# A two-layer conditioned convolution and expert layer: the opening in another order

## The reference

```python
# layer 0
c0 = grouped_conv1d(x, weight, taps=9, groups=4) + (cond @ c_weight.T)[:, :, None] + side[None, :, None]
x1 = x + experts(c0; layer 0)
# layer 1: each sample has its own 32x32 mixing matrix
h   = gelu(gelu(cond @ W0 + b0) @ W1 + b1)
att = softmax(h @ W2 + b2)                      # 128 x 8
c1  = einsum('boi,bih->boh', einsum('bk,koi->boi', att, weight), x1) + (att @ bias_k)[:, :, None]
out = x1 + experts(c1; layer 1)

# experts(y): each of the 4096 rows of 512
logits = y @ W_router.T                         # 8 experts, the best 2, softmax over them
out = y @ W_base.T + b_base + 2 * sum over the best 2 of gate_e * (y @ A_e.T) @ B_e.T    # rank 16
```

## Time and profile before

| | us |
|---|---|
| median of three runs | 392.79 |
| the profiled execution's own time | 393.22 |
| its span in the trace | 391.4 |
| TensorE busy | 375.9 (96%) |
| VectorE busy | 206.6 (53%) |
| GpSimd busy | 169.9 (43%) |
| ScalarE busy | 125.6 (32%) |
| mean granted TensorE clock | 0.978 |

### The profile page before, as it was taken

The page is one execution under the profiler, slowest core; times in us unless marked ns, Lnnn a source line. Parts: engine busy times, 40 slices in busy tenths (PEclk is TensorE's granted clock), DMA queues, the critical chain, the costliest instruction groups (busy, mean ns, idle before and its releaser), DMA issues.

```text
span 391.4 us, 8410 instructions
## 1 busy us (share of the span) xinstructions
PE 375.9 (96%) x2648; PEld 365.4 (93%) x2648; DVE 206.6 (53%) x837; ACT 125.6 (32%) x374; POOL 169.9 (43%) x136
## 2 busy tenths in 40 slices
PE   8785999999999999999999999999999999999996
PEld 6465899999999999999999999999999999999896
DVE  2935355545555455555565455555554555555545
ACT  2631323332333233322333233323332333223331
POOL 3172155335533554345434553455335543454450
PEclk9868799999999999999999999999999999999999
DMA  7986223444433433443433443444334334433101
GB/s 258 308 240 172 95 76 127 122 149 123 147 113 114 147 121 122 146 147 121 117 119 139 132 135 121 147 124 144 116 112 147 121 121 147 145 123 107 54 28 54
DMA packets 45019, 51.91 MB, mean 133 GB/s; under 512 B 11280, under 2 KB 27440, under 8 KB 45008
## 3 DMA queue, kind: packets, MB, share of 16 engines
q1 hardware_dynamic: 45008, 51.78, 41.7%
HBM read 34.70 MB, written 17.06 MB: 132 GB/s over the span
## 4 chain that ended last, share of the span: by engine, by line
PE 89%; SPq 3%; DMA 3%; DVE 2%; issue 1%; ACT 0%; DVEq 0%; ACTq 0%
PE ps_out L398 35%; PE ps_out L410 22%; PE ps_out L432 11%; PE ps_conv L353 7%; PE ps_mix L446 7%; PE ps_conv L358 4%; DMA y_scratch<-y 1%; SPq L292 1%; PE ps_out L453 1%; PE ps_t L419 1%; PE ps_out L419 1%; DMA x_raw<-in_x_phase 1%; DMA scratch<-mix_nat 1%; SPq L309 1%; SPq L304 1%
## 5 line engine op out<-in xcount | busy, mean ns | idle before, releaser
L398 PE MATMUL ps_out<-wa,yT 128*128 128x392 f32 x756 | 154.8, 352 | 1.5 <-DVE res L817 0.8
L398 PEld LDWEIGHTS ps_out<-wa,yT 128*128 128x128 f32 x756 | 130.7, 190 | 4.0 <-DVE res L817 1.3
L410 PE MATMUL ps_out<-wb,yT 128*128 128x256 f32 x756 | 102.9, 285 | 0.0
L410 PEld LDWEIGHTS ps_out<-wb,yT 128*128 128x128 f32 x756 | 94.3, 190 | 0.0
L953 POOL TENSOR_TENSOR yT<-y_raw,yT 128x512 fp32r<-128x512 f32 x31 | 39.5, 1274 | 97.5 <-ACT yT L549 97.5
L964 POOL TENSOR_TENSOR base_bias<-passed,bias 128x512 f32<-128x512 f32 x31 | 39.9, 1288 | 95.8 <-ACT passed L600 95.8
L432 PE MATMUL ps_out<-lb_w,hwT 128*128 128x256 f32 x384 | 56.2, 282 | 0.8 <-ACT hwT L549 0.8
L432 PEld LDWEIGHTS ps_out<-lb_w,hwT 128*128 128x128 f32 x384 | 52.1, 189 | 1.4 <-issue 0.8
L959 POOL TENSOR_TENSOR xb<-x_tok,bias 128x512 f32<-128x512 f32 x32 | 41.0, 1283 | 10.0 <-DMA bias<-in_bias 10.0
L549 ACT ACTIVATE hwT<-ps_t 128x128 fp32r<-128x128 f32 x32 | 8.9, 278 | 103.7 <-PE ps_t L419 103.7
L781 DVE MAX8 top<-ps_out 128x8 f32<-128x8 f32 x64 | 10.8, 169 | 58.9 <-issue 57.4
(11 more groups left out here) (101 smaller groups left out, 339.4 us busy)
## 6 DMA issues: line engine op xcount, KB each, us to landing
x_raw<-in_x_phase SPq DMA_DIRECT2D x31, 384.0 KB, 3.2
x_tok<-in_x_tok SPq DMA_DIRECT2D x32, 256.0 KB, 2.6
y_scratch<-y SPq DMA_DIRECT2D x31, 256.0 KB, 2.3
y_raw<-y_scratch SPq DMA_DIRECT2D x31, 256.0 KB, 2.7
out<-res SPq DMA_DIRECT2D x31, 256.0 KB, 2.0
wa_raw<-in_wa SPq DMA_DIRECT2D x2, 784.0 KB, 4.9
wb_raw<-in_wb SPq DMA_DIRECT2D x2, 512.0 KB, 5.7
lb_raw<-in_lb SPq DMA_DIRECT2D x2, 256.0 KB, 4.9
```

The source lines that it names most:

```text
L398: last = mm(out_banks(y, t)[:, 0, 0:AR + DH], features(y, t, dp)[:, k, :], wa[y][:, wp, k, :], start=(n == 0 and k == 0), stop=(n == len(S ...
L410: last = mm(out_banks(y, t)[:, 1, OUT], features(y, t, dp)[:, k, :], wb[y][:, wp, k, :], start=(n == 0 and k == 0), stop=False, skip_group ...
```

## The change

SyncE issues `x_raw` for tile 1 and all loads behind it without waiting for `x_first`, which gets a semaphore of its own. `x_raw` of tiles 2 and 3, `y` of tiles 1 and 2, the layer 1 weights, the four `mix` rows, the broadcasts, `lb1` and `bias1` stand in another order. The biases of all samples are made by a third product of their own, from a copy of the condition in which the samples are sorted by their place in the tile, so that each broadcast reads one whole run of 4 KB. The products for tiles 0 and 1 and their addition come first. TensorE runs conv(1) ahead of `kernel_scores`, has two of its nine dummy products later, and transposes the probabilities ahead of the last quarter of tile 0's first product. Tile 0's low-rank transpose uses another bank and comes ahead of its second product. GpSimd makes four of the sixteen sorting copies (ScalarE five instead of seven, VectorE seven instead of nine). VectorE and ScalarE split the weights in another order.

```diff
+POOL_MOVES = [(2, 2), (2, 3), (3, 2), (3, 3)]
...
 @block.sync
-            sp.dma_start(x_first[:, :, :], d["x_phase"][0]).then_inc(x_loaded, 16)
+            sp.dma_start(x_first[:, :, :], d["x_phase"][0]).then_inc(x_first_loaded, 16)
             sp.dma_start(pack[:, :], d["pack"]).then_inc(l_pack, 16)
-            sp.wait_ge(x_loaded, 16)
             sp.dma_start(x_raw[:, :, :], d["x_phase"][1]).then_inc(x_loaded, 16)
...
             sp.dma_start(bias[0][:, :], d["bias0"]).then_inc(l_bias[0], 16)
-            sp.wait_ge(cb_ready, 1)
+            load_x(2)
+            store_y(1)
+            sp.dma_start(wa_raw[1][:, :, :], d["wa1"]).then_inc(l_wa[1], 16)
+            load_y(1)
+            sp.dma_start(wb_raw[1][:, :, :], d["wb1"]).then_inc(l_wb[1], 16)
+            sp.wait_ge(cb_ready, 2)
             sp.dma_start(d["bias_scratch"], some_bias[:, 2, :]).then_inc(bias_stored, 16)
-            store_y(1)
-            load_weights(1)
-            load_y(1)
-            sp.wait_ge(bias_stored, 16)
-            for n in range(SPT):
-                sp.dma_start(conv_bias[n::SPT, :, :],
-                             d["bias_scratch"][n::SPT, :].unsqueeze(0).to_broadcast([NB, TILES, C])
-                             ).then_inc(l_bias_conv, 16)
-            sp.dma_start(lb_raw[1][:, :], d["lb1"]).then_inc(l_lb[1], 16)
-            sp.dma_start(bias[1][:, :], d["bias1"]).then_inc(l_bias[1], 16)
-            load_x(2)
             load_tok(1)
...
+            sp.wait_ge(bias_stored, 16)
+            for n in range(SPT):
+                sp.dma_start(conv_bias[n::SPT, :, :],
+                             d["bias_scratch"][n * TILES:(n + 1) * TILES, :].unsqueeze(0).to_broadcast([NB, TILES, C])
+                             ).then_inc(l_bias_conv, 16)
+            load_x(3)
+            store_y(2)
             sp.dma_start(d["scratch"], mix_nat[:, :]).then_inc(mix_stored, 16)
+            load_y(2)
+            sp.dma_start(lb_raw[1][:, :], d["lb1"]).then_inc(l_lb[1], 16)
+            sp.dma_start(bias[1][:, :], d["bias1"]).then_inc(l_bias[1], 16)
             sp.wait_ge(mix_stored, 16)
...
-            store_y(2)
-            load_y(2)
-            load_x(3)
+            store_y(3)
             load_tok(2)
-            store_y(3)
             load_y(3)
 @block.tensor
-            keep_busy(9)
+            keep_busy(7)
             conv(0)
...
-            pe.wait_ge(cond_ready, 2)
-            for n, cond in enumerate((some_cond[:, 0, :], some_cond[:, 1, :], condT)):
-                last = mm(ps_mix[:, 0, n * C:(n + 1) * C], cond, cw_sb, start=True, stop=True)
-            last.then_inc(cb_mm, 1)
+            pe.wait_ge(cond_ready, 3)
+            for n in range(2):
+                biases_product(n, some_cond[:, n, :]).then_inc(cb_mm, 1)
...
+                biases_product(2, some_cond[:, 2, :]).then_inc(cb_mm, 1)
...
+            conv(1)
             kernel_scores()
-            conv(1)
-            first_product_0()
-            turn_probabilities()
+            keep_busy(2)
+            first_product_0(before_last=turn_probabilities)
             mixing_setup()
+            pe.wait_ge(cb_ready, 2)
+            turn_hw(0, 0)
             second_product_0()
-            turn_hw(0, 0)
             b_product(0, 0)
 @block.scalar
-            for n in range(SPT - 1):
-                move_first(3, n)
+            move_first(3, 0)
             probabilities()
             high_wa_part(0, FIRST_KS)
             high_wa_part(0, LAST_KS)
             high_wb(0)
+            high_lb(0)
             weigh(0, 0)
-            high_lb(0)
...
+            turned_hw(0, 0)
             high_y(1)
-            turned_hw(0, 0)
 @block.vector
-            for n in range(SPT):
-                move_first(2, n)
-            move_first(3, SPT - 1)
+            move_first(2, 0)
+            move_first(2, 1)
+            move_first(3, 1)
             scores()
             conv_out(1)
             probabilities()
+            turned_probabilities()
+            choose(0, 0)
+            biases(2, 1, 2)
             low_wa_part(0, FIRST_KS, 1)
-            turned_probabilities()
+            gate(0, 0)
             low_wa_part(0, LAST_KS, 2)
-            choose(0, 0)
-            low_wb(0)
-            gate(0, 0)
             mixing_biases()
             low_lb(0)
             turned_hw(0, 0)
-            low_wa_part(1, FIRST_KS, 1)
+            low_wb(0)
             middle(0)
             conv_out(2)
-            low_wa_part(1, LAST_KS, 2)
+            low_wa_part(1, FIRST_KS, 1)
             choose(0, 1)
             turned1(0)
             gate(0, 1)
+            low_wa_part(1, LAST_KS, 2)
             low_wb(1)
             conv_out(3)
 @block.gpsimd
+            pool.wait_ge(s["y0"], 1)
+            for n, (q, sample) in enumerate(POOL_MOVES):
+                need(pool, pool_moved, n)
+                dst, src = first_move(q, sample)
+                g.tensor_copy(dst, src).then_inc(pool_moved, 1)
...
             form_xb(0)
-            low_y(1)
             pool.wait_ge(l_wa[1], 16)
             g.tensor_tensor(k_sums[:, :, 0:AR + DH], wa_raw[1][:, 0:2, :], wa_raw[1][:, 2:4, :],
                             ALU.add).then_inc(k_summed, 1)
+            low_y(1)
             pool.wait_ge(l_wb[1], 16)
```

More of the change, by code:

```diff
@@ L115, in build @@
             pack[:, int(at[k]):int(at[k]) + n] for k, n in PACK.items())
-        some_cond = sb("some_cond", [P, 2, P])
+        some_cond = sb("some_cond", [P, 3, P])
         some_bias = sb("some_bias", [P, 3, C])
@@ L212, in stages, with turned @@
             at(LAST - 1)
+        def turned(y, t):
+            return ps_hwT[1] if isinstance(t, int) and t == 0 else ps_hwT[y]
         def out_banks(y, t):
@@ L350, in conv @@
                 need(pe, s["y0"], t)
-                pe.wait_ge(x_loaded, 16 * (t + 1))
+                if first:
+                    pe.wait_ge(x_first_loaded, 16)
+                else:
+                    pe.wait_ge(x_loaded, 16 * t)
                 for g in range(GROUPS):
@@ L361, in conv, with first_product_0 @@
                 last.then_inc(s["conv"], 1)
-            def first_product_0():
+            def first_product_0(before_last):
                 pe.wait_ge(l_wa[0], 16)
-                pe.wait_ge(moved, MOVES)
+                pe.wait_ge(moved, MOVES - len(POOL_MOVES))
+                pe.wait_ge(pool_moved, len(POOL_MOVES))
                 for k in range(KT):
+                    if k == KT - 1:
+                        before_last()
                     last = mm(ps_out[0][:, 0, 0:AR + DH], y_first[:, k, :], wa_raw[0][:, k, :],
@@ L418, in turn_hw @@
                     pe.wait_ge(sums_ready, 2)
-                mm(ps_hwT[y], hw[y][:, :], ident, is_transpose=True, start=(y == 1), stop=True,
+                mm(turned(y, t), hw[y][:, :], ident, is_transpose=True,
+                   start=(y == 1 or isinstance(t, int) and t == 0), stop=True,
                    skip_group_check=True).then_inc(s["hwt"][y], 1)
@@ L453, in keep_busy, with biases_product @@
                     mm(ps_out[0][:, 0, :], zeros[:, 0:P], zeros[:, :], start=True, stop=True)
-            keep_busy(9)
+            def biases_product(n, cond):
+                return mm(ps_t0[:, (n + 4) * C:(n + 5) * C], cond, cw_sb, start=True, stop=True)
+            keep_busy(7)
             conv(0)
@@ L605, in turned_hw @@
                 need(act, s["b"][y], t)
-                copy(hwT[y][HI][:, :], ps_hwT[y]).then_inc(s["hwh"][y], 1)
+                copy(hwT[y][HI][:, :], turned(y, t)).then_inc(s["hwh"][y], 1)
             def turned1(t):
@@ L704, in _, with biases @@
                           condT[:, SPT:2 * SPT].unsqueeze(1).to_broadcast([P, NB, SPT])).then_inc(cond_ready, 1)
-            dve.wait_ge(cb_mm, 1)
-            v.tensor_tensor(some_bias[:, :, :], ps_mix[:, 0, 0:3 * C].rearrange("p (a c) -> p a c", c=C),
-                            side_sb.unsqueeze(1).to_broadcast([P, 3, C]), ALU.add).then_inc(cb_ready, 1)
+            v.tensor_copy(some_cond[:, 2, :].rearrange("p (n t) -> p n t", t=TILES),
+                          condT.rearrange("p (t n) -> p n t", n=SPT)).then_inc(cond_ready, 1)
+            def biases(first, count, n):
+                dve.wait_ge(cb_mm, first + count)
+                v.tensor_tensor(some_bias[:, first:first + count, :],
+                                ps_t0[:, (first + 4) * C:(first + count + 4) * C].rearrange("p (a c) -> p a c", c=C),
+                                side_sb.unsqueeze(1).to_broadcast([P, count, C]), ALU.add).then_inc(cb_ready, 1)
+            biases(0, 2, 1)
             def scores():
@@ L807, in turned_hw @@
                 dve.wait_ge(s["hwh"][y], t + 1)
-                low(hwT[y][LO][:, :], ps_hwT[y], hwT[y][HI][:, :].bitcast(F32)).then_inc(s["hwl"][y], 1)
+                low(hwT[y][LO][:, :], turned(y, t), hwT[y][HI][:, :].bitcast(F32)).then_inc(s["hwl"][y], 1)
             def halves(features):
@@ L980, in _ @@
```

(5 more changed lines are left out.)

3 lines of the change are left out of this document (2 added, 1 removed).

## The result

The changed kernel took 388.15 us (median of four runs, 387.19 to 389.38) against 392.62 for the kernel before beside it: a ratio of 0.9877 [0.9843 to 0.991]. A second set on another occasion gave 387.33 against 393.33, 0.9872 [0.9833 to 0.9911]. The gain is 4.5 to 6 us where 9 were forecast; the time lies inside the range, the size of the gain does not lie near the forecast.

The account below looks back on a forecast made before the run. It took the opening before `first_product(0, 2)` to be bound by SyncE's queue order; moving that start from 49.30 to 40.15 us gains 9.15, giving 383.7 us after the profile and median offsets, 80% range 379.8 to 388.5.

Parts of the forecast that it names:

- Step 1: Start of the opening: loads without waits, seven dummy products; first copies into `y_first` at 9.13, 0.5 us earlier.
- Step 2: Sorting copies: GpSimd's four at 0.35 us each; all copies end at 11.4, between 10.9 and 12.2.
- the 384.5 by that rule: Sorting copies under the full VectorE/GpSimd port lock: copies end near 12.2, the sum becomes 384.5 us.
- Step 3: Scores and probabilities ahead: `att_mT` near 14.5, kernel products at full clock, 1.7 us, ending 17.15.
- Step 4: SyncE's queue: `mix` rows from 17.9 instead of 23.58; whole-line broadcasts issue in 0.5 us each, landing at 24.4.
- B: Broadcasts no cheaper: landing at 29.8 pushes the later steps by 5.4 us; 389.1 us, chance 0.06.
- D: Slower through SyncE's queue: work waits for broadcasts landing at 39.1; 398 us, chance 0.04.
- Step 5: Tile 2: conv(2) lies under the broadcast, so half clock costs nothing; `conv_out(2)` ends at 25.15.
- Step 6: End of opening: `bias1` lands last, at 31.9 after 3.15 us, delaying GpSimd; `first_product(0, 2)` at 40.15 instead of 49.30.
- A: `bias1` not last; product chain and ScalarE's order set `first_product(0, 2)` at 36.9; 380.4 us, chance 0.12.
- C: Half clock or dearer copies in a further place, such as conv(3): 387 us, chance 0.12.

Follow-up runs that it names:

- experiment 1: The changed kernel timed and profiled again with no edit, against the kernel before: 387.33 us, ratio 0.9872.
- experiment 3: Changed kernel with the loads of `lb1` and `bias1` issued early, right behind the layer 1 weights `wb1`: 384.17 us, ratio 0.9762 to the kernel before.
- experiment 6: Changed kernel with no sorting copies on GpSimd, VectorE making nine and ScalarE seven as before: 387.58 us, ratio 0.9871 to the kernel before.
- experiment 7: Changed kernel with `lb1` and `bias1` issued between `load_x(3)` and `store_y(2)`: 383.42 us, ratio 0.9752 to the kernel before.
- experiment 10: Changed kernel with nine dummy products at the start and `bias1` loaded right behind `bias0`: 382.69 us, ratio 0.9753 to the kernel before.
- experiment 2: Changed kernel with nine dummy products at the start instead of seven: 386.48 us, ratio 0.9833 to the kernel before.
- experiment 5: Changed kernel with the broadcasts read in broken lines, 128 bytes at a time as before: 388.58 us, ratio 0.9896 to the kernel before.
- experiment 9: Changed kernel with the four transfers of `mix` from `scratch` moved behind `store_y(3)`: 387.21 us, ratio 0.9853 to the kernel before.
- experiment 11: Changed kernel with the edits of experiment 9 and experiment 10 together: 383.56 us, ratio 0.9757 to the kernel before.
- experiment 12: Experiment 10 with the conv bias stored as soon as made and its broadcasts ahead of the `mix` rows: 381.87 us, ratio 0.972 to the kernel before.
- experiment 8: The kernel of experiment 7 with nine dummy products at the start: 382.58 us, ratio 0.974 to the kernel before.

## Why the forecast was right in kind and half wrong in size

**Step 1** failed by omission. The 0.5 us, and more, was there in experiment 1's execution (first copies at 8.69 where the forecast had 9.13, before 9.63). What I priced at nothing is the clock: behind seven dummy products TensorE stood idle until `x_first` landed (0.54 us in the profile after, 0.38 in experiment 1), and the rise to 2.4 GHz came at 14.25 in the first and at 5.55 in the second. The idle time alone does not make the rise late: experiments 3, 6 and 7 had 0.51 to 0.53 us of it and rose at 4.30 to 5.71. Eight profiles of kernels with seven dummies show it at 4.30, 4.62, 5.55, 5.71, 5.77, 6.53, 6.92 and 14.25; six with nine at 4.51 to 6.88. So the late rise was seen once in eight, and why it came there stays open. It cost 2.9 us up to the `mix` rows in that execution. In the mean two pairs put nine dummies 0.85 us below seven, and the kernel before shows nothing; whether seven costs anything in the mean is not settled.

**Step 2** held: the price was right (0.335 us a copy, estimate 0.35), and the sharing was worth nothing, as experiment 6 shows and the forecast's own 11.4 implied (nine copies from 9.13 on end at 11.35). Seven copies took 2.04 us beside GpSimd's, 2.27 by the forecast and 1.73 without contention; had the eleven taken turns it would have been 3.1. So the lock that the Trainium skill describes (page "SBUF — State Buffer", section "SBUF: two separate sides") does not show in full on these copies, and the 384.5 by that rule would have rested on the wrong term. It does show on operations of two SBUF inputs: `lb_w` took 2.14 us beside `k_sums` in the profile after; in experiment 10 it started 0.09 us ahead of `k_sums`, took 0.68, and `k_sums` 2.32 instead of 1.92. Whoever starts first goes through, as that section of the Trainium skill says.

**Step 3** held where the clock allowed it. In experiment 1 `att_mT` ran at 13.78 (forecast about 14.5), and the kernel products at full clock. That full clock is luck of the execution: in five other profiles (experiments 2, 5, 9, 11 and 12) the clock fell at 16.7 to 17.2, in the middle of those products, and stayed at half for 6.8 us (in experiment 7 at 17.95, for 3.4 us), and two of the first four executions of the changed kernel had a mean clock of 0.982, no better than the kernel before (0.978 to 0.983). ScalarE's first weight split stands ahead of its tanh in the kernel, not behind it as the diff above prints; it ran inside that engine's wait (at 11.95 in the profile after, the tanh at 14.44).

**Step 4** held in sum: 0.59 us an issue instead of 0.5, and the last landing 24.9 (forecast 24.4). Its reason was the smaller part: whole lines save 1.2 us, the place in the queue 2.3 (experiment 5). Rivals B and D were priced with the old train at 9.3 us, and it took 8.1.

**Step 5** held: `conv_out(2)` at 25.03 in experiment 1 for 24.46, 0.6 late with the broadcasts. That half clock costs nothing there did not hold: in experiments 2, 9, 11 and 12, at half clock up to 23.6 to 24.0, SyncE waited for conv(2) before it could issue `x_raw` for tile 3, at 24.7 to 25.1 (22.90 in experiment 1), and tile 2's `y`, stored behind that load, took 3.6 to 5.3 us to land (2.7 in experiment 1). No run changes this alone, so its price at the end is not shown.

**Step 6** is the step that failed in size. The mechanism is exactly the one named: `bias1`, then `base_bias`, `xb(1)`, `low_y(2)`, `conv_out(3)`, `first_product(0, 2)`; experiment 3 takes `bias1` out and 3.2 us go. The term that was mis-sized is its landing. I took 3.15 us, near the 2.6 of `x_tok`; the changed kernel took 4.6 and 3.9. There it is the third of three 256 KB loads issued within a microsecond and has four transfers behind it; which of these makes it late was not separated (experiment 9). `x_tok`'s row is a median over the even stretch, where only the end of one other load runs beside it. The 4.9 of the old `bias` was no price of this load either: it is the middle of two, and the view of `bias` in the kernel before has the other ends:

```profile
DMA to landing us min/median/max: 3.7/4.9/6.1
```

The least is `bias1`, issued right behind `lb1` then as now; with 3.7 the forecast would have been 0.55 us nearer. The miss is then the sum of terms: in experiment 1, 0.55 (broadcasts) + 1.5 (landing) + 0.15 = 2.2 us, 42.37 for 40.15; in the profile after, 2.9 (clock) + 0.6 (broadcasts) + 0.75 (landing) + 0.2 = 4.45, 44.60 for 40.15.

**The rivals.** A (380.4, `bias1` not last) had the size nearly right and the limit not: with `bias1` removed as the last, `first_product(0, 2)` began at 38.0 in experiments 8 and 10 where A had 36.9, and the medians of experiments 7, 8, 10, 11 and 12 are 381.9 to 383.6. What set it there was tile 2's round trip of `y`, not ScalarE's order. C (half clock in a further place) came, but in the first convolutions, a place that it did not name. The half clock behind the wait for `bias1` (12 products in 2.76 us, 1.59 where the clock stayed at 1.00) was in the sum, in step 6. B and D did not happen.

## What to carry to other kernels

Where a load becomes the last thing a stage waits for, take its landing time from a row with the same company in the queue (how much was issued just ahead of it and just behind), not from the median of that transfer in an even loop. When a queue is reordered, look for the small load that everything behind waits for and send it early; how early matters only until the next thing is late. And work that only keeps an engine busy may have a price when it is removed: check in more than one profile what the clock does, before a stretch at full or at half clock is put down to the change.

## What the runs showed of the hardware

TensorE's clock rose at 14.25 us in one execution of the changed kernel and at 5.55 in another of the same program, with 0.54 and 0.38 us of idle time ahead of the first convolution; the first one ended 2.0 us later (388.57 and 386.55). With the same program on TensorE up to there, the clock fell to half at 16.77 in experiment 9 and not before 36.27 in experiment 1; up to 16.77 TensorE had last stood idle for 0.40 us in the one, ahead of 13.79, and for 0.41 us in the other, ahead of 13.46. Behind TensorE's waits of 3.84 us (profile after) and 4.55 us (experiment 1) the granted clock was at half, and the twelve products of the second half took 2.76 us, where experiment 10, whose clock did not fall in the opening, has 1.59. A 32 by 128 copy in float32 took GpSimd 0.335 us and VectorE 0.246.
